# Starting the first step on half of the weights, and moving x's maxima within VectorE's order

## The reference

```
x: (32, 128, 2048)   idx: (32,)   cond: (32, 128, 128)
W: (2048, 2048)  b: (2048,)  gate: (8, 2048)  A: (8, 16, 2048)  B: (8, 2048, 16)

w   = cond[idx]
y   = einsum('bct,bcd->bdt', x, w)                   # per batch a 128x128 product
res = einsum('bnd,od->bno', y, W) + b
route_w = top-2 of softmax(y @ gate.T), renormalised
h   = einsum('bnd,erd->bner', y, A)
out = x + res + einsum('bner,eor->bno', h * route_w, B)
```

## Time and profile before

| | |
|---|---|
| median of 3 timed runs | 1682.91 us (1681.62 to 1683.14) |
| profiled execution | 1682.7 us |
| its span, first to last instruction | 1680.9 us |
| mean granted TensorE clock | 0.974 of full speed |
| busy: TensorE, VectorE | 1536.2 us (91%), 1310.5 us (78%) |
| busy: ScalarE, GpSimd | 593.9 us (35%), 603.9 us (36%) |
| DMA | 201.87 MB, mean 120 GB/s |

### The profile page before, as it was taken

How to read it: one execution, slowest core, us unless ns; L and a number is a source line. 1 busy time by engine, 2 the same in 40 slices (tenths; PEclk the granted TensorE clock), 3 DMA queues, 4 the chain that set the end, 5 groups by cost and what they waited for, 6 DMA issues and landing times.

```text
span 1680.9 us, 25726 instructions
## 1 busy us (share of the span) xinstructions
PE 1536.2 (91%) x9539; PEld 833.5 (50%) x9539; DVE 1310.5 (78%) x2234; ACT 593.9 (35%) x996; POOL 603.9 (36%) x467
## 2 busy tenths in 40 slices
PE   5369999999999999999668999999999999999998
PEld 4355445555555555555464445545545554554553
DVE  4677777787777777777767888888888888888875
ACT  6563333333333333333583322332332233232231
POOL 2244555555555555555452122211212221221222
PEclk9589999999999999999889999999999999999999
DMA  5243443444434444444621244433324433333432
GB/s 196 79 141 110 124 129 123 132 132 130 130 125 131 132 132 127 122 129 125 224 101 55 82 128 132 119 108 119 99 85 132 132 113 114 115 90 98 132 104 69
DMA packets 102911, 201.87 MB, mean 120 GB/s; under 512 B 10874, under 2 KB 24186, under 8 KB 102266
## 3 DMA queue, kind: packets, MB, share of 16 engines
q1 hardware_dynamic: 102786, 200.22, 38.6%
HBM read 128.96 MB, written 71.22 MB: 119 GB/s over the span
## 4 chain that ended last, share of the span: by engine, by line
PE 75%; DVE 13%; issue 6%; ACT 4%; DMA 1%; POOL 0%; SPq 0%; POOLq 0%; DVEq 0%; ACTq 0%
PE bank_y L995 9%; PE bank_y L996 9%; PE bank_y L994 9%; PE bank_x L994 9%; PE bank_x L996 8%; PE bank_x L995 8%; DVE amax L659 4%; PE bank_z L996 3%; PE bank_z L995 3%; PE bank_z L994 3%; DVE t_sums L716 3%; PE bank_c L994 2%; PE bank_c L995 2%; PE bank_c L996 2%; ACT TT L516 1%
## 5 line engine op out<-in xcount | busy, mean ns | idle before, releaser
L429 POOL TENSOR_TENSOR x_res<-x_res,t_sums 128x512 f32<-128x512 f32 x256 | 340.2, 1329 | 963.0 <-DVE t_sums L720 809.3
L994 PE MATMUL bank_x<-TT,s_parts 128*128 128x512 f16 x768 | 292.9, 381 | 13.4 <-POOL TT L413 7.4
L995 PE MATMUL bank_x<-TT,s_parts 128*128 128x512 f16 x768 | 292.6, 381 | 0.0
L996 PE MATMUL bank_x<-TT,s_parts 128*128 128x512 f16 x768 | 292.6, 381 | 0.0
L995 PE MATMUL bank_y<-TT,s_parts 128*128 128x512 f16 x768 | 291.1, 379 | 0.0
L996 PE MATMUL bank_y<-TT,s_parts 128*128 128x512 f16 x768 | 291.1, 379 | 0.0
L994 PE MATMUL bank_y<-TT,s_parts 128*128 128x512 f16 x768 | 291.0, 379 | 0.0
L506 ACT ACTIVATE p_copies<-bank_x,y_inv 128x512 f32<-128x512 f32 x128 | 87.4, 683 | 435.2 <-PE bank_x L996 346.1
L491 ACT ACTIVATE s_parts<-a_full 128x512 f16<-128x512 f32 x224 | 141.0, 630 | 270.8 <-DVE a_full L698 123.3
L720 DVE TENSOR_TENSOR t_sums<-t_sums,inv_w 128x512 f32<-128x512 f32 x256 | 223.3, 872 | 8.8
L693 DVE TENSOR_TENSOR s_parts<-a_full,s_parts 128x512 f16<-128x512 f32 x224 | 192.0, 885 | 3.0 <-ACT s_parts L491 3.0
(11 more groups left out here) (214 smaller groups left out, 2720.4 us busy)
## 6 DMA issues: line engine op xcount, KB each, us to landing
x<-in_x_dram SPq DMA_DIRECT2D x32, 1024.0 KB, 5.6
x_res<-in_x_dram SPq DMA_DIRECT2D x128, 256.0 KB, 3.7
part_scratch<-x_res SPq DMA_DIRECT2D x128, 256.0 KB, 2.7
x_res<-part_scratch SPq DMA_DIRECT2D x128, 256.0 KB, 4.0
out_dram<-x_res SPq DMA_DIRECT2D x128, 256.0 KB, 2.9
x_res<-in_L_ffn_W_base_dram SPq DMA_DIRECT2D x12, 512.0 KB, 4.5
w_cond<-in_L_cond_weights_dram SPq DMA_DIRECT2D x64, 64.0 KB, 3.9
a_full<-in_L_ffn_W_base_dram SPq DMA_DIRECT2D x8, 512.0 KB, 5.0
```

The lines of the kernel that those rows point to most:

```text
L429: nc.gpsimd.tensor_tensor(XR[:, xr_slot(m), :], XR[:, xr_slot(m), :], TM[:, m % 2, :], ALU.add).then_inc(r_added, 1)
L994: nc.tensor.matmul(dst, lhs[0], rhs[0], start=start, stop=False, skip_group_check=chained)
L995: nc.tensor.matmul(dst, lhs[0], rhs[1], start=False, stop=False, skip_group_check=chained)
L996: return nc.tensor.matmul(dst, lhs[1], rhs[0], start=False, stop=stop, skip_group_check=chained)
```

## The change

Two things are changed.

**The first step.** The queues are written anew up to the end of step 0. The maxima, the split and the cond products of step 0's x stand between units 0 to 3 of the weights. Once these four units and the seven S operands are ready, product(0, 0, 0) to (0, 0, 6) run, and between them the transposes of A, B and gate. F's sums and its lower parts move from VectorE to GpSimd (split_f_lo). Then the features of step 0, units 4 to 7, and product(0, 1, q) with the cond products of step 1. Rows of units 0 to 3 are staged in XR slots 2 to 5 and the bias's memory, those of units 4 to 7 in AF and XP; units 4 to 7 turn over two PSUM banks instead of five, as the other banks hold tiles of step 0.

**The maxima.** find_maxima(n + 1) no longer opens step n; find_maxima(n + 2) stands after s_lower(n + 1, S3) and before finish(n, 1, C12).

The diff, cut to its core:

```
+        def bank_of(g, i):
+
+            if NU // 2 <= g < NU:
+                return (BX[1], BD)[i % 2]
+            return (BX[0], BX[1], BY[0], BY[1], BZ)[(4 * (g % NU) + i) % 5]
...
+        early_rows = [xr_rows[:, 1, :], xr_rows[:, 2, :], bias[:, 0:KH], bias[:, KH:2 * KH]]
+        late_rows = [af_rows[:, 0, :], af_rows[:, 1, :], xp_rows[:, 0, :], xp_rows[:, 1, :]]
...
+            sp.wait_ge(cond_done, 4)
+            sp.wait_ge(s_lo, NPROD)
+            load_rows(4)
+            load_rows(5)
+            for m in range(4):
+                store_tile(m)
+                if m > 0:
+                    sp.wait_ge(xr_out[xr_slot(m - 1)], xr_turn(m - 1))
+                    load_tile(m - 1 + NXR)
+            sp.wait_ge(f_lo, 2)
+            sp.dma_start(ft_dram, FT_second.rearrange("p f s n -> p (f s n)")).then_inc(ft_out, 16)
+            sp.wait_ge(b_lo, 1)
+            sp.dma_start(bt_dram, BT_first).then_inc(bt_out, 16)
...
+            for g in (6, 7):
+                sp.wait_ge(w_tr, 4 * (g - 1))
+                load_rows(g)
...
+            pool.wait_ge(a_copied, 4)
+            pool.wait_ge(f_full, 2)
+            for k in range(2):
+                ins = nc.gpsimd.tensor_tensor(F21[k], F12[k][:, C4:2 * C4, :], F12[k][:, 0:C4, :], ALU.subtract)
+            ins.then_inc(f_sum, 1)
+            add_r(1)
+            split_f_lo(0, FT[:, :, :, :])
+            add_r(2)
+            add_r(3)
+            split_f_lo(1, FT_second)
...
-            for n in range(NSTEP):
+            for n in range(1, NSTEP):
                 more, second = n + 1 < NSTEP, n >= NP
-                if more:
-                    find_maxima(n + 1)
                 features(n)
...
                 if more:
                     s_lower(n + 1, S4)
                     s_lower(n + 1, S3)
+                if n + 2 < NSTEP:
+                    find_maxima(n + 2)
                 finish(n, 1, C12)
...
+                    back = 2 if NU // 2 <= g < NU else 5
+                    owner, eldest = 4 * g + i - back, 4 * (NU // 2) if NU // 2 <= g < NU else 4 * (g // NU) * NU
+                    if owner >= eldest:
                         before, what = owner // 4, owner % 4
...
+            pe.wait_ge(w_lo, 3 * (NU // 2))
+            pe.wait_ge(w_sum_lo, 4 * (NU // 2))
+            product(0, 0, 0)
+            pe.wait_ge(agb_diag, 2)
+            pe.wait_ge(af_copied, 4)
...
+            for q in range(1, 5):
+                product(0, 0, q)
+                transpose_a_and_b(q - 1)
```

More of the change, by code:

```diff
@@ L540, in _, with lift_s @@
             act.wait_ge(consts, E + 2)
+            def lift_s(n, u, q):
+                copy_a(n, u)
+                s_upper(n, q)
             sum_rows(0)
+            sum_rows(1)
+            w_upper(0)
+            split_x_hi(0, 0)
+            split_x_hi(0, 1)
+            sum_rows(2)
+            w_upper(1)
+            lift_s(0, U_A11, A11)
+            sum_rows(3)
+            w_upper(2)
+            lift_s(0, U_S1, S1)
+            lift_s(0, U_A12, A12)
+            w_upper(3)
+            s_upper(0, S2)
+            lift_s(0, U_A22, A22)
+            s_upper(0, S4)
+            s_upper(0, S3)
             act.wait_ge(a_in, 16)
@@ L546, in _, with copy_features @@
                                  accum_out=agb_sum[0:E, 1:2]).then_inc(agb_sums, 1)
-            sum_rows(1)
-            w_upper(0)
-            act.wait_ge(agb_spread, 1)
-            nc.scalar.copy(inv_ag[:, :], BC[:, 0:HW]).then_inc(agb_inv, 1)
-            for j in range(4):
+            def copy_features(j):
                 act.wait_ge(a_tr, j + 1)
@@ L856, in agb_scales @@
                 link(nc.vector.reciprocal(agb_rpow2[0:p, :], agb_pow2[0:p, :]))
[L858 to L865 removed]
             dve.wait_ge(consts, E + 2)
             w_scales(0)
+            find_maxima(0)
+            find_top(0)
+            w_scales(1)
+            w_sums_and_lower(0)
+            scale_x(0)
+            split_x_lo(0, 0)
+            split_x_lo(0, 1)
+            w_scales(2)
+            w_sums_and_lower(1)
+            s_lower(0, A11)
+            w_scales(3)
+            w_sums_and_lower(2)
+            s_lower(0, S1)
+            sum_s2(0)
+            s_lower(0, A12)
+            w_sums_and_lower(3)
+            s_lower(0, S2)
+            sum_s4_s3(0)
+            s_lower(0, A22)
+            s_lower(0, S4)
+            s_lower(0, S3)
             agb_scales(0)
@@ L895, in _ @@
                     b_transposed.rearrange("q (k p j) -> q j k p", k=4, j=NJ)[:, C4 * j:C4 * (j + 1), :, :],
-                    quads(BD[:, :]).rearrange("q c (k p) -> q c k p", k=4)).then_inc(b_copied, 1)
-            w_sums_and_lower(2)
+                    quads(BX[1][:, :]).rearrange("q c (k p) -> q c k p", k=4)).then_inc(b_copied, 1)
+            copy_b(0)
+            finish(0, 0, C11)
+            copy_b(1)
+            copy_b(2)
+            copy_b(3)
+            finish(0, 0, C12)
+            finish(0, 0, C21)
+            finish(0, 0, C22)
             agb_scales(2)
@@ L902, in _ @@
                                     ALU.mult, ALU.mult).then_inc(agb_diag, 1)
+            find_maxima(1)
             dve.wait_ge(b_hi, 1)
@@ L927, in _ @@
             w_sums_and_lower(7)
-            for n in range(NSTEP):
+            scale_x(1)
+            split_x_lo(1, 0)
+            split_x_lo(1, 1)
+            s_lower(1, A11)
+            finish(0, 1, C11)
+            s_lower(1, S1)
+            sum_s2(1)
+            s_lower(1, A12)
+            s_lower(1, S2)
+            sum_s4_s3(1)
+            s_lower(1, A22)
+            finish(0, 1, C12)
+            s_lower(1, S4)
+            s_lower(1, S3)
+            find_maxima(2)
+            finish(0, 1, C21)
+            finish(0, 1, C22)
+            for n in range(1, NSTEP):
                 more, second = n + 1 < NSTEP, n >= NP
-                if more:
-                    find_maxima(n + 1)
                 features(n)
```

247 lines of the change are left out of this document (121 added, 126 removed).

## The result

The changed kernel takes 1666.40 us, median of four runs (1664.65 to 1668.70), against 1682.74 for the kernel before on the same chip (1681.62 to 1683.14): ratio 0.9905, 95% interval 0.9888 to 0.9922. Forecast 1666.8.

A forecast was written before the change was run, and what follows sets the result against it. TensorE bounds the steps, while chains between ScalarE, VectorE and GpSimd set the preparation. 1682.7 − 23.35 (maxima) + 7.3 (first step) = 1666.65, predicted as 1666.8 us; own range 1662 to 1671, 8 in 10 for 1657 to 1675.

The forecast's parts named there:

- The waits go: Moved maxima remove the transpose's wait in both halves, no new wait; second half's w_cond_parts wait grows from 0.80 to 1.0 us.
- What a wait costs: TensorE's waits for the maxima priced at its idle time: 18.3 us for 15 waits in steps 1 to 15.
- part 1: The moved maxima: −18.3 − 5.9 + 0.85 = −23.35 us, between −17.4 and −26.2.
- First product at 55.0: Step 0's first product starts at 55.0 us instead of 118.95, after GpSimd's lower parts of unit 3.
- TensorE waits until 62.0: After product 0 ends at 58.9 us, TensorE waits until 62.0 for A's and gate's sums and VectorE's scales.
- part 2: The rewritten first step: step 0 ends at 169.65 instead of 162.30, +7.3 us; +1.4 to +14 by cases.
- I add nothing: F's moved split meets C21, C22 of step 0: 1 to 2 us on VectorE within 3.0 us of slack, uncharged.
- The rule of the Trainium skill: GpSimd splits could hold VectorE twice, 4.8 us in all; late units start 1.8 us later, 1668.5 in all.
- Stores: SyncE writes F out at 99.9 and B at 100.3; B takes 6.0 us, so unit 4's w_upper starts at 106.3.
- Late units: Units 4 to 7 on two PSUM banks run from 106.3 to 146.4; step 0's second half starts at 147.6.
- Opening of the weights' second half, +0.85: Step 15's maxima now precede its last tiles, so the second half of the weights opens 0.85 us late.
- Rival 2: Part 2 worse by 7 us: GpSimd and VectorE block each other at 85 to 106, late stores, slower units; 1674, chance 0.15.

The follow-up runs named there:

- four-edit kernel: Kernel after with GpSimd's bias held back, five-bank ring for units 4 to 7, second half's scaling and split of x first, C11's addition held back: 1635.15 us, ratio 0.9724.
- lower parts first: Kernel after with GpSimd making the second lower parts of A and gate before adding product tiles 2 and 3, stores moved ahead too: 1666.12 us, ratio 0.9902.
- scaling first: Kernel after with VectorE scaling the next step's x before finishing C11 in the second half's steps: 1667.03 us, ratio 0.9909.

## Why the prediction was right, and by what luck

The total is right to 0.4 us by luck, twice: the errors of the two parts cancel down to 2.0 us (1666.65 forecast, 1664.65 in the profiled execution, whose marks follow), and the median lies 1.75 us above that execution. By the marks, forecast against measured: step 0 and its prologue +6.1 (7.3, less step 1's wait) against +9.8; steps 2 to 15 −17.1 against −19.3; the opening of the weights +0.85 against −0.6; steps 17 to 30 −5.9 against −7.9. By kernels that do one part: −23.35 against −28.2, and +7.3 less 1.2 against +9.7.

- **The waits go.** Right in both halves, and no new one. In the second half TensorE's w_cond wait grew to 1.02 us as forecast (13.2 us over 13 in 960 to 1640), so its idle time fell by 0.40 a step where I had 0.42.
- **What a wait costs.** The mis-sized term of part 1. I priced each at the idle time that the row of TensorE's matmuls gives (1.22 us). Periods say 43.48 − 42.10 = 1.38. With 47.50 as the period without waits, all five kernels agree, each for one window of 13 steps: two waits, idle 1.42, cost 1.76; one wait, idle 1.02, cost 1.19; 0.79, cost 0.97; 0.31, cost 0.48. Each wait costs 0.16 to 0.18 us more than its idle time. Over 14 steps of either half that is 2.2 and 2.4 us, which nearly fill the 4.8 us between forecast and measured for part 1 alone. Two other terms of that kernel nearly cancel. Mark 2 comes 0.1 us earlier where the forecast has 1.2, for its TensorE came to the higher clock at 124.0 us and the kernel before at 121.6. And marks 16 to 17 are 0.8 us shorter where the forecast has them 0.85 longer. The row of the weight loads is no better guide: its idle time is right in the first half (1.40) and 0.32 too long in the second (1.51 for 1.19, 0.80 for 0.48), where its differences hold but not its size. That is why the four-edit kernel won 0.48 us a step and not 0.80.
- **First product at 55.0.** 54.45. The layout of the queues was good to 1% there, and product 6 ended at 89.4 for 87.2.
- **TensorE waits until 62.0.** This step failed: 65.21. I looked for the meeting of GpSimd and VectorE only between 85 and 106 us, and the bias additions, moved to 54 us by the change, met five of VectorE's operations that I priced at their undisturbed length. Holding them back gives 2.8 us. These are not simply 2.8 of the 3.7 us by which part 2 was short, since units 4 and 5 made up the delay against the forecast (see late units).
- **"I add nothing" for the moved split of F.** Half wrong. B's lower part took 4.16 us (98.34) where the earlier trace rows have 2.35, and C22's second operation 2.09 for 0.69:

```profile
92.51 2.09 DVE L793 TENSOR_TENSOR t_sums<-t_sums,inv_w 128x512 f32<-128x512 f32 x1
...
98.34 4.16 DVE L987 SCALAR_TENSOR_TENSOR TT<-TT,b_scale 128x2048 f16<-128x2048 f32 x1
```

  The rule of the Trainium skill that I set aside (SBUF — State Buffer, Who interferes with whom: a VectorE operation with two SBUF inputs and a reading GpSimd operation exclude each other for a whole instruction) is borne out by this trace: here, at 54 us, at 145 us (below) and in the second half's steps. By that rule the forecast was 1668.5, farther from the total but nearer for the part. Yet the place of the split in GpSimd's order was worth little: with it and the stores ahead, mark 2 moved 0.3 us. No run has the split back on VectorE, so what the move itself cost is not shown.
- **Stores.** Issued at 103.60 for 99.9, but B's landed in time for 109.5 (forecast 106.3): 5.5 us, and not 6.0.
- **Late units.** Sums of unit 6 begin at 117.51 (116.65 to 118.95), of unit 7 at 128.75 (129.3), second half of step 0 at 151.03 (147.6). Unit 4 began 3.2 us late, and units 4 and 5 took 10.3 and 11.3 us where I had 12.65 each, so ScalarE ended unit 7 at 146.38, for 146.4. The 3.4 us of this stage were lost behind that, by GpSimd's four lower parts of unit 7, of which I had added one. TensorE began when the last was done:

```profile
144.90 2.82 POOL L436 TENSOR_TENSOR TT<-p_copies,TT 128x512 f16<-128x512 f32 x2 [3.11 <-ACT TT L587]
147.68 3.24 POOL L436 TENSOR_TENSOR TT<-t_sums,TT 128x512 f16<-128x512 f32 x2
```

  They took 6.0 us; those of unit 6 took 4.5 (from 137.30). VectorE's scaling and splitting of step 1's x lies beside them and took longer too (2.09 us at 147.82 for 1.28, 1.23 at 149.84 for 0.35). This is the mis-sized term of part 2: of the 3.4 us about 1.8 are my own count and 1.5 exclusion, by these rows; no run tests it. The cost of two banks was in the forecast as a longer chain, and I took it for the price of the early start. It was the price of an assignment of banks: 9.9 us with the other one.
- **Opening of the weights' second half, +0.85.** The stage itself is 0.43 us longer (73.33, where the earlier trace rows have 72.90) and TensorE's way to it 0.2. The rest is the clock: it rose 2.9 us after the first product of step 16, and 5.5 us after it in the kernel before.

Rival 2's mechanism (the engines holding one another up) was real, at half its price, and met also before and behind the stretch where I looked.

## What to carry to other kernels

Test a change of two parts by its parts: this one's −16 is −28 and +10, and the +10 turned into a gain of 2 once the early work had its banks and GpSimd's additions were held back. When an operation is moved to another engine or another place, list what it now runs beside, at every point, and look at both engines' rows there. An instruction of a few numbers that takes a microsecond is a waiting one, and a chain through it can be shortened by delaying an engine that has time.

## What the runs showed of the hardware

- **Exclusion works for tiny operations too.** VectorE's scale of 128x4 numbers, with one SBUF input, took 1.12 us beside GpSimd's addition and 0.17 without. Not all are held up: the reciprocal of 128x4 numbers keeps its 0.18 us, ahead of GpSimd's addition as here (by 0.04 us) or within a GpSimd operation, as at 145.73 (the operation runs from 144.90 to 146.06). So do operations with one number a partition: tensor_scalars at 94.53, 94.70 and 95.09 in the kernel after took 0.14 to 0.15 us within GpSimd's split (1.66 us from 94.02). The maxima's reduction took 2.27 us everywhere, with GpSimd at work beside it (95.68 in the kernel after) or not. Who comes first holds the other back: GpSimd 2.17 us for 1.27, VectorE 1.36 for 0.35. The Trainium skill (same section) says that tensor_scalar can contend as well as operations with two SBUF inputs, that issue order decides who blocks, and that tensor_reduce doesn't on trn2; the trace agrees on all three.
- **A wait of TensorE costs its idle time and 0.16 to 0.18 us**, by the periods of five kernels.
- **The clock at step 16 differs from run to run of the same code.** TensorE comes to step 16 from idle time (7.46 us before 878.73 in the kernel after, 5.88 in the other below), and its products are then 0.43 us apart (1.2 GHz) until the clock rises and they are 0.22 apart (2.4 GHz). Timelines of TensorE there, in the kernel after and in the one with the lower parts first, which has the same code from step 1 on:

```profile
878.73 0.59 PE L1083 MATMUL bank_x<-TT,s_parts 128*128 128x512 f16 x1 [7.46 <-POOL TT L436]
...
881.25 0.58 PE L1083 MATMUL bank_x<-TT,s_parts 128*128 128x512 f16 x1
881.66 0.38 PE L1084 MATMUL bank_x<-TT,s_parts 128*128 128x512 f16 x1
```

```profile
878.65 0.58 PE L1084 MATMUL bank_x<-TT,s_parts 128*128 128x512 f16 x1 [5.88 <-issue]
...
883.29 0.63 PE L1086 MATMUL bank_x<-TT,s_parts 128*128 128x512 f16 x1
883.72 0.32 PE L1084 MATMUL bank_h<-FT,s_parts 128*128 128x136 f16 x1
...
884.51 0.29 PE L1085 MATMUL bank_h<-FT,s_parts 128*128 128x136 f16 x1
```

The clock rose 2.9 us into the step in the first and 5.9 in the second; the stretch from mark 16 to 17 took 118.57 and 120.28 us, 1.7 us by luck. The idle time isn't what decides: in the kernel with the scaling first it is 7.46 us too, and the clock rises after 5.1 us. The same is seen at the first product of step 0, with 7.44 and 7.46 us of idle time before it: the clock rises after 2.7 us in the kernel before and 4.8 in the one with only the maxima moved. The kernel after probably had that luck in its profiled execution (mean clock 0.971, in the other three 0.968 and 0.969, of which there are no traces), so its trace says −18.0 where the medians say −16.3.
